# Masked attention on one core: the sums beside the values move behind two groups of projections, in front of the scores

## What is computed

```python
def attention(q, k, v, mask):                      # 16 heads of 16 columns
    scores = jnp.einsum('bhqd,bhkd->bhqk', q, k) / jnp.sqrt(jnp.float32(HD))
    scores = scores * mask - 10000.0 * (1.0 - mask)
    probs = jax.nn.softmax(scores, axis=-1)
    return jnp.einsum('bhqk,bhkd->bhqd', probs, v)
ln_out = layernorm(hidden_states, ln1_s, ln1_b)
q, k, v = jnp.split(ln_out @ w_qkv + b_qkv, 3, axis=-1)
ctx = merge_heads(attention(split_heads(q), split_heads(k), split_heads(v), ltor_mask))
x = hidden_states + ctx @ w_ao + b_ao
...
ctx = merge_heads(attention(..., cross_mask))      # keys and values from the context
x = x + ctx @ w_co + b_co
```

## Time and profile before

| What | Value |
|---|---|
| median of 3 runs | 2274.27 us (2271.91 to 2277.16) |
| the profiled execution | 2272.06 us |
| its span | 2270.3 us, mean granted TensorE clock 0.992 |
| TensorE busy over the span | 2179.0 us (96%), 17621 matmul records |
| VectorE, ScalarE, GpSimd busy | 1554.7, 1573.0, 725.4 us (68%, 69%, 32%) |
| scores of the masked stage (L1295) | 256 records, 1468.8 to 1818.4 us |

### The profile page before, as it was taken

One profiled execution on the slowest core, in us unless ns is written; L12 is line 12 of the kernel. 1 busy time (PEld: TensorE's weight loads), 2 busy tenths in 40 slices (PEclk: granted clock), 3 DMA queues, 4 the chain that ended last, 5 costly groups with the idle time before them and its releaser, 6 DMA issues. The chain is left out here.

```text
span 2270.3 us, 51859 instructions
## 1 busy us (share of the span) xinstructions
PE 2179.0 (96%) x17621; PEld 1779.6 (78%) x17621; DVE 1554.7 (68%) x3940; ACT 1573.0 (69%) x4479; POOL 725.4 (32%) x885
## 2 busy tenths in 40 slices
PE   8999999999999999998999999889999989999998
PEld 7899999998999999997985666556666679766664
DVE  6555555567555555557759999687776676899985
ACT  4666666665667666665737777577788776578875
POOL 2211111123211111102124655377777720233201
PEclk9999999999999999999989999999999999999999
DMA  5100112010010000002000000100000000000001
GB/s 135 24 25 24 24 25 61 24 24 1 24 24 25 24 24 24 1 1 64 11 8 11 11 9 6 39 8 2 6 15 17 14 8 5 7 11 11 7 4 38
DMA packets 72945, 47.16 MB, mean 21 GB/s; under 512 B 29232, under 2 KB 71600, under 8 KB 72752
## 3 DMA queue, kind: packets, MB, share of 16 engines
q1 hardware_dynamic: 70576, 43.57, 7.3%
q10 hardware_dynamic: 2176, 1.05, 0.2%
HBM read 41.45 MB, written 2.10 MB: 19 GB/s over the span
## 5 line engine op out<-in xcount | busy, mean ns | idle before, releaser
L2155 DVE TENSOR_REDUCE maxima<-bank 128x2 f32<-128x512 f32 x512 | 332.6, 681 | 30.4 <-PE bank L1103 28.3
L1715 ACT ACTIVATE probs_t<-bank 128x512 f32<-128x512 f32 x512 | 282.4, 601 | 64.8 <-PE bank L1092 63.4
L2011 DVE SCALAR_TENSOR_TENSOR wide_heads_low<-bank,wide_columns,wide_heads_high 128x128 fp32r<-128x128 f32 x512 | 155.8, 346 | 209.3 <-ACT wide_heads_high L1580 209.2
L1568 ACT ACTIVATE wide_probs<-bank,wide_neg_max 128x129 f32<-128x129 f32 x512 | 184.2, 365 | 118.7 <-DVE wide_neg_max L1991 114.4
L1563 ACT ACTIVATE wide_probs_t<-bank 128x256 f32<-128x256 f32 x256 | 98.3, 384 | 161.7 <-PE bank L959 159.5
L2512 POOL TENSOR_TENSOR wide_columns<-wide_pair_columns,zero 128x8 f32<-128x8 f32 x16 | 3.3, 209 | 640.7 <-DVE x L2024 638.9
L1995 DVE RECIPROCAL wide_inverse<-wide_sums 128x2 f32<-128x2 f32 x256 | 42.4, 166 | 227.7 <-ACT wide_probs L1568 227.7
L1574 ACT ACTIVATE wide_probs<-wide_probs,wide_inverse 128x128 f32<-128x128 f32 x448 | 156.1, 396 | 52.0 <-DVE wide_inverse L1995 52.0
L1092 PE MATMUL bank<-q_packed,k_packed 32*128 32x256 f32 x1024 | 167.6, 330 | 7.5 <-ACT probs_t L1715 6.8
L1103 PE MATMUL bank<-k_packed,q_packed 32*128 32x256 f32 x1024 | 172.6, 334 | 2.2 <-DVE maxima L2155 1.1
L1752 ACT ACTIVATE probs<-scores_masked,neg_max 128x128 f32<-128x128 f32 x512 | 163.2, 394 | 10.7 <-DVE neg_max L2334 10.0
(11 more groups left out here) (319 smaller groups left out, 6799.5 us busy)
## 6 DMA issues: line engine op xcount, KB each, us to landing
cn<-in_ctx SPq DMA_DIRECT2D x48, 128.0 KB, 2.1
q_packed<-max_rows SPq DMA_DIRECT2D x256, 4.0 KB
wide_pair_weights<-in_L_xattn_wq SPq DMA_DIRECT2D x15, 256.0 KB, 2.7
wide_pair_weights<-in_L_xattn_wk SPq DMA_DIRECT2D x15, 256.0 KB, 3.2
wide_pair_weights<-in_L_xattn_wv SPq DMA_DIRECT2D x15, 256.0 KB, 3.5
wide_pair_weights<-in_L_xattn_wo SPq DMA_DIRECT2D x15, 256.0 KB, 3.3
x<-in_x SPq DMA_DIRECT2D x4, 512.0 KB, 7.1
wide_ctx_rows<-in_ctx SPq DMA_DIRECT2D x4, 512.0 KB, 8.7
```

Of the source, the lines that this page charges most:

```text
L1568: last = act.activation(probs0[:, b, h, :], wide_scores[b % 2][:, h * KEYS0:(h + 1) * KEYS0], ACT.Exp, bias=neg_max0[:, b, h:h + 1], accum ...
L1715: act.activation(probs_t[j % 8][:, :], shifted_bank[j % 2][:, :], ACT.Exp, bias=0.0).then_inc(s.exp_ready, 1)
L2011: last = dve.scalar_tensor_tensor(heads_low[:, h, a, :], wide_heads[a % 2][:, h * P:(h + 1) * P], columns[slot][:, 3, h:h + 1], heads_high ...
L2155: dve.tensor_reduce(maxima[pack // 2][:, b, pack % 2, :], head_scores[packed_scores(1 - u, j)][:, :].rearrange("p (a k) -> p a k", a=UNITS ...
```

## The change

Only TensorE's order inside a window changes; the instructions, their data, their waits and the other four engines' programs are the same.

- The group of transposes of step 1 moves behind the heads and the keys.
- The sums of steps 0 and 1 move behind the transposes of the tail, to the end of step 1.
- The sums of step 2 move from the end of step 2 to step 3, where they follow those of step 3 in one group of 16 records, at the window's end.
- The values move behind the queries.

```diff
@@ -1294,13 +1294,6 @@
                             half = slice(r * P // 2, (r + 1) * P // 2)
                             pe.matmul(score_bank[r][:, :], qk[u][half, j // 2, :], km[u][half, j // 2, :], start=True, stop=True)\
                               .then_inc(s.scores, 1)
-                    if core and j == 3 or past and j < 3:
-                        pe.wait_ge(s.exp_ready, g - 2)
-                        after(pe, s.probs_copied, g - 3)
-                        t = (j - 3) % STEPS
-                        for m in range(PACK):
-                            last = pe.transpose(turn_bank[:, m * P:(m + 1) * P], probs[t][:, m * P:(m + 1) * P], ident[:, :])
-                        last.then_inc(s.probs_turned, 1)
                     if late and j == 1:
                         pe.wait_ge(s.heads_taken, n - 2)
                         if core:
@@ -1318,6 +1311,13 @@
                                 last = pe.matmul(project2_bank[:, m * P:(m + 1) * P], w_qkv[:, layer, c, m * P:(m + 1) * P],
                                                  keys_of[:, c, :], start=c == 0, stop=c == DC - 1)
                         last.then_inc(s.projected, 1)
+                    if core and j == 3 or past and j < 3:
+                        pe.wait_ge(s.exp_ready, g - 2)
+                        after(pe, s.probs_copied, g - 3)
+                        t = (j - 3) % STEPS
+                        for m in range(PACK):
+                            last = pe.transpose(turn_bank[:, m * P:(m + 1) * P], probs[t][:, m * P:(m + 1) * P], ident[:, :])
+                        last.then_inc(s.probs_turned, 1)
                     if late and j == 2:
                         layer = late[0]
                         pe.wait_ge(s.heads_copied, n - 2)
@@ -1327,15 +1327,6 @@
                         last.then_inc(s.result, 1)
                         if isinstance(n, int) and n == 2 * B + 1:
                             turn_hidden(ROUNDS)
-                    for t in (0, 1) if past and j == 1 else (j,) if past and j else ():
-                        pe.wait_ge(s.probs_copied, g - j + t - 3)
-                        if t == 0:
-                            pe.wait_ge(s.v_ready, n)
-                            after(pe, s.sums_copied, n - 1)
-                        for m in range(PACK):
-                            last = pe.matmul(sums2_bank[m * QUAD:(m + 1) * QUAD, t * P:(t + 1) * P], vn[1 - u][:, 0, PACK * t + m, :],
-                                             probs_t[t][:, m * P:(m + 1) * P], start=True, stop=True)
-                        last.then_inc(s.sums, 1)
                     if ahead and j == 0:
                         layer, b = ahead
@@ -1358,15 +1349,6 @@
                         for m in range(STEPS):
                             last = pe.transpose(unturned_bank[:, m * P:(m + 1) * P], sums_copy[:, m, 0:P], ident[:, :])
                         last.then_inc(s.sums_turned, 1)
-                    if soon and j == 3:
-
-                        layer, b = soon
-                        keys_of = cn_t[1 - u] if layer else rows_t[1 - u]
-                        after(pe, s.x_added, n - 2)
-                        for c in range(DC):
-                            last = pe.matmul(rows_bank, keys_of[:, c, :], w_qkv[:, layer, c, 2 * D:3 * D],
-                                             start=c == 0, stop=c == DC - 1)
-                        last.then_inc(s.values, 1)
                     if ahead and j == 3:
                         layer = ahead[0]
                         pe.wait_ge(s.in_ready, n + 3)
@@ -1375,6 +1357,24 @@
                             for c in range(DC):
                                 pe.matmul(project2_bank[:, m * P:(m + 1) * P], w_qkv[:, layer, c, m * P:(m + 1) * P],
                                           rows_t[u][:, c, :], start=c == 0, stop=c == DC - 1)
+                    if soon and j == 3:
+
+                        layer, b = soon
+                        keys_of = cn_t[1 - u] if layer else rows_t[1 - u]
+                        after(pe, s.x_added, n - 2)
+                        for c in range(DC):
+                            last = pe.matmul(rows_bank, keys_of[:, c, :], w_qkv[:, layer, c, 2 * D:3 * D],
+                                             start=c == 0, stop=c == DC - 1)
+                        last.then_inc(s.values, 1)
+                    for t in (0, 1) if past and j == 1 else (2, 3) if past and j == 3 else ():
+                        pe.wait_ge(s.probs_copied, g - j + t - 3)
+                        if t == 0:
+                            pe.wait_ge(s.v_ready, n)
+                            after(pe, s.sums_copied, n - 1)
+                        for m in range(PACK):
+                            last = pe.matmul(sums2_bank[m * QUAD:(m + 1) * QUAD, t * P:(t + 1) * P], vn[1 - u][:, 0, PACK * t + m, :],
+                                             probs_t[t][:, m * P:(m + 1) * P], start=True, stop=True)
+                        last.then_inc(s.sums, 1)
             over_sequence(pe, window)
```

More of the change, by code:

```diff
@@ L1360, in window @@
                         last.then_inc(s.sums_turned, 1)
+                    if ahead and j == 3:
+                        layer = ahead[0]
+                        pe.wait_ge(s.in_ready, n + 3)
+                        after(pe, s.qk_ready, n + 2)
+                        for m in range(DC):
+                            for c in range(DC):
+                                pe.matmul(project2_bank[:, m * P:(m + 1) * P], w_qkv[:, layer, c, m * P:(m + 1) * P],
+                                          rows_t[u][:, c, :], start=c == 0, stop=c == DC - 1)
                     if soon and j == 3:
@@ L1369, in window @@
                         last.then_inc(s.values, 1)
[L1370 to L1374, removed]
-                            for c in range(DC):
-                                pe.matmul(project2_bank[:, m * P:(m + 1) * P], w_qkv[:, layer, c, m * P:(m + 1) * P],
-                                          rows_t[u][:, c, :], start=c == 0, stop=c == DC - 1)
+                    for t in (0, 1) if past and j == 1 else (2, 3) if past and j == 3 else ():
[7 more added lines that the diff above has]
+                        last.then_inc(s.sums, 1)
             over_sequence(pe, window)
```

## The result

| | before | after |
|---|---|---|
| median, 20 runs each | 2274.10 us (2271.61 to 2277.16) | **2279.24 us** (2276.32 to 2282.53) |
| ratio | | 1.0022 (95%: 1.0015 to 1.0029) |
| profiled execution | 2272.06 us | 2278.25 us |
| its span, mean granted clock | 2270.3 us, 0.992 | 2276.5 us, 0.986 |

A forecast was written before the change was run, and what follows sets the result against it. TensorE was taken to carry the masked stage, with new waits for VectorE's reads limiting the gain. Steady part -5.2 us and fill +3.8 gave -1.4 on 2272.06, or 2273 from the median: no difference; range 2267 to 2279.

The forecast's parts named there:

- The steady window: Masked stage: first half 5.00 us against 5.33, second 5.69 against 5.76; odd windows gain 0.40, even ones 0.07.
- The loop windows: Windows 19 to 26, 11.17 us each before: put at no change, 0.2 each way.
- The last two windows: End of the masked stage: with no queries to wait for, a gain of 1.2 us.
- Fill: +3.8 us: Windows -1 to 2: values behind the queries no longer fill TensorE's waits; a loss of 3.8 us in all.
- +1.3: Window -1: values at the lower clock cost 1.7 us, half a microsecond comes back; net loss 1.3.
- a spell of 1.1: Window 0: longer idle time may lower TensorE's clock again, costing 0 to 2 us; 1.1 taken.
- Window 1, "+0.6": Fill: scores come 2.65 us after VectorE's read instead of 2.08, a loss of 0.6.
- Window 2, "+0.6": Fill: taken as of the same kind as window 1, a loss of 0.6 us.
- The second: Rival: the queries' wait makes the kernel slower; even and loop windows slip by 0.5, or fill loses clock twice: 2282; chance 0.13.
- The third: Rival: waits and transposes leave TensorE too idle, so its clock falls in the steady stage: 2286 us; chance 0.03.
- The first: Rival: waits for VectorE are shorter than 0.15 us and the fill keeps its clock: 2267; chance 0.22.
- The signs of being wrong: Waits staying with L1758; even windows below 10.8; clock under 1.00 after 1500 us; window 3's scores over 5 later or unmoved.

The follow-up runs named there:

- e3: The changed kernel with the values in front of the queries again in all windows, sums still last: 2277.56 us (ratio 1.0015 to the kernel before).
- e5: The changed kernel with unread idle matmuls in front of the queries' waits of windows -2, -1, 0 and 2: 2273.7 us (1.0001 to the kernel before).
- e10: The kernel before with only the values moved behind the queries in windows -1 to 2: 2279.71 us (1.0022).
- e2: New order in windows -4 to 2, old order in all others: 2280.5 us (1.0033 to the kernel before).
- e1: Old order in windows -4 to 2, new order from window 3 on: 2271.43 us (0.9990 to the kernel before).
- e11: The changed kernel with the values back in front of the queries in windows -1 to 2: 2271.15 us (0.9987 to the kernel before).
- e8: e1 with all sums of steps 2 and 3 before queries and values, and keys before the heads: 2252.84 us (0.9905 to the kernel before).
- e12: The changed kernel measured once more, unaltered: 2278.61 us (1.0018 to the kernel before).

## Why the prediction was wrong

**The steady window was right.** First half 5.00 predicted, 5.01 measured. Second half 5.69 in odd windows, 5.69 measured; even windows of 11.02 in all, 10.97 measured (5.01+5.96). Windows 4 and 6 should lose 0.32: 11.97 against 11.65. Windows 5 and 7 gained the 0.34 that I had put (10.75 against 11.09); window 3, which begins in a low spell, only 0.05. Both waits stand where they were forecast, and the rule that carried it, next scores 2.65 us behind VectorE's read, holds to the hundredth.

**The loop windows were right only in sum.** Put at no change, they take 10.90 (odd) and 11.35 (even) against 11.17: -0.27 and +0.18. The last two windows were put at -1.2, "with no queries to wait for"; they gained 0.13 (window 30, 10.07 against 10.20) and 0.32 (window 31's first half, 4.11 against 4.43). In window 30 the values wait 0.30 for VectorE's addition to x (L2314), the wait of e3. In all the steady part gained 4.6 us where 5.2 were forecast.

**The step that failed is "Fill: +3.8 us".** Its mechanism was right, its size was not: the fill lost 6.65. By its terms, each against the starts in the earlier trace rows and after:

- Values at half clock in window -1, "+1.3" net, and "+0.2" and "a spell of 1.1" in window 0, 2.6 together: measured +2.4 and +1.3, 3.7 (the half microsecond that was to come back did: the read of window 0 ends 0.66 sooner after the scores, and is in the +1.3). The values took 1.85 where I counted 1.7, and the queries ahead of them 1.84 against 1.35 before, which I left out: the first spell had begun long before them. In window 0 I took the middle of 0 to 2 for a spell; queries and values both fell wholly into it, 1.75.
- Window 1, "+0.6": measured 0.94. The order gave 0.57, and its scores, begun at half clock, 0.37.
- Window 2, "+0.6": measured 2.05. The order gave 0.76, a third spell 1.3. I had not foreseen that TensorE would stand idle for 2.13 us there. Before, it had values and a group of sums to do in that time. Nor was this window "of the same kind" as window 1: its scores before came 1.89 after the read, not 2.08.

So of an error of 2.85 us in this term, nearly all is the clock: the order's part came out at 2.1 us where the forecast's terms have 2.3 (0.86, 0.2, 0.6, 0.6), but I priced half clock for one group of values and one new spell, 1.9 us, and in the reading above 4.8 us are lost at the lower clock. e5 confirms it by giving back 4.6 of the loss in the trace and 5.5 in the medians.

**The sum.** With the measured terms, 6.65-4.31-0.32 = +2.0 us in this stage, where -1.4 was forecast. In the two profiled executions the rest of the 6.2 us is 2.65 ahead of the first rows turned and 1.5 behind the last scores. Ahead the code is the same in all 13 profiled executions, and they turn their first rows at 1460.94 to 1464.70; the one of before is the earliest. Behind, from the last scores to the end, they take 450.5 to 455.1; before and after are level up to the feed-forward part (18.74 and 18.73 us from the last scores to L807) and part only in code that is the same. What differs there between before and after is again the clock (windows view, before, then after):

```profile
1170.00:1200.00 30.00, 26.79 (x180) 19.12 (x178) 25.08 (x56) 13.90 (x27) 12.08 (x21) 0.77 0.04 11
1950.00:2000.00 50.00, 46.95 (x420) 31.46 (x416) 43.70 (x108) 33.39 (x68) 17.44 (x24) 0.90 0.04 11
```

```profile
1170.00:1200.00 30.00, 27.20 (x157) 19.29 (x159) 23.76 (x55) 13.34 (x24) 12.01 (x21) 0.72 0.05 15
1950.00:2000.00 50.00, 47.09 (x389) 32.56 (x387) 40.59 (x101) 30.82 (x62) 16.06 (x22) 0.86 0.03 8
```

By the medians the difference is 5.1 (3.4 to 6.6), some 3 us more than the stage's. The execution of before was 2.0 below its median, that of after 1.0 below. Over all runs whose clock is on record the granted clock has a median of 0.990 before and 0.985 after, and single executions with the same figure take about the same time: at 0.987, 2278.4 to 2278.7 before and 2277.2 to 2277.5 after; at 0.988, 2277.2 and 2277.5 against 2276.3 and 2276.4. So what the changed kernel loses in the median goes with the lower clock. Where the low clock of the 3 us falls in the median execution, and whether the order brings it about there, isn't shown: one execution of before and two of the changed kernel have a profile. Open too is what sets the length of the first spell: it lasted 10.2 us in the changed kernel and in e10, 3.4 in e2, whose windows in the fill are those of the changed kernel, and 6.8 in e1 against 3.4 before, whose fill is the same.

**The rivals.** The second, slower, named "or the fill loses its clock twice" as a side term and let the even and loop windows carry it; the even loop windows slipped by 0.18, the odd ones gained 0.27 and the even ones from 8 to 18 0.1, where it wanted a slip of 0.5. It came out on its side by the term I treated as minor. The third, a clock that falls in the steady stage, did not happen beyond the first microsecond of window 3: 1.00 from 1515 to 1810. The first was wrong in both of its conditions: releases reach TensorE in 0.14 to 0.15 (1507.46 to 1507.60; one of 0.05 stands in e3, behind L2314), and the fill did not keep its clock. The Trainium skill (TensorE: Matmul & The Clock Gate, Part 4) says that transposes do not count as busy for the gate. The prediction said that the trace speaks against this; it does not test it. A steady window has 24 transposes (26 with context rows; 16 to 18 was a miscount), but they stand among keys, queries, values, sums and scores, and no run has a long stretch of transposes alone.

**The signs of being wrong.** Two of those named beforehand came: a granted clock under 1.00 after 1500 us (the third spell, from 1508.6), and first scores of window 3 later by more than 5 us (1511.40 against 1502.10, 6.65 of it in the fill). The last scores, forecast 1 us earlier than 1818, came at 1822.50.

**What I should have read.** In the trace before, the values stood in windows -1 and 0 where TensorE would otherwise wait, and so cost little and kept it busy. Moving them behind the wait does two things: it puts up to 0.96 on the path, and it lengthens the idle time (2.71 to 3.58 in window 0, none to 2.13 in window 2), and the low clock that followed fell on exactly the work behind it. I priced the second in window 0 alone. A stretch of 2% of the span decided the sign.

## What to carry to other kernels

Work that can run before a wait belongs before it, even where TensorE has air: in the fill of a pipeline, 0.96 us of values behind the wait instead of in front of it cost 1.1 (e10) to 1.6 us a window (the changed kernel against e11), the larger part through the clock. Price a change of order separately for the fill and the steady part; a gain of 0.15 a window over 28 windows is lost by four windows that pay 1.7. Where waits for a bank bound a half, look at which engine frees it and how late, and place next to the wait the largest piece that waits for nothing (here 16 sums and the keys: 18.6 us together, e1 to e8).

## What the runs showed of the hardware

- **Run-to-run spread goes with the granted clock.** Single executions of the kernel before took 2272.0 us at a mean granted clock of 0.992, 2274.0 at 0.990, 2277.5 at 0.988; of the changed kernel 2277.2 at 0.987, 2278.2 at 0.986, 2280.9 at 0.984. From the first to the last of each that is 1.4 and 1.2 us for each 0.001.
- **A low spell costs by what stands in it, not by its length.** e1 has 10.2 us of low clock in the fill and loses 0.4 us against the kernel before with 3.4; the changed kernel has 20.4 and loses 4.8 against full clock. The difference is whether queries, values and sums behind the awaited read fall into the spell or a wait does.
- **Idle matmuls in four short waits returned 5.5 us** of 2279 (4.9 against e12), with no other edit.
- **A change of tile shape costs about 0.15 us.** This is an estimate from the earlier trace rows (two groups of 8 sums 0.72, one of 16 0.57; four transposes 0.59 between other shapes, 0.44 inside a run); the forecast built on it met the measured halves (5.00 and 5.69 against 5.01 and 5.69), and no run varies the changes of shape alone. Transposes behind keys (1613.79 to 1614.68 for eight records of keys, 0.89) cost nothing extra, the upper bound of 0.1 a window was not needed.
